# A fourth place for attention probabilities, a seventh addend for GpSimd in six narrow steps, and later projections in an eight-sample U-net block

## What is computed

```
block 0:  x  = x + proj(attention(group_norm(x)))            8 heads of 32 channels
block 1:  a  = group_norm(x) + pos;  gate = sigmoid(conv(silu(conv3x3(silu(conv(a))))))
          sh = group_norm(a);  enh = a * gate
          std = attention(sh, sh, sh)                          8 heads of 32
          mul = [attention(enh, sh, sh)] * 2                   2 heads of 128
          x   = x + group_norm(ff(silu(ff1([std, mul]))))
block 2:  xn = group_norm(x);  x = xn + proj(attention(xn))    8 heads of 32
block 3:  x  = x + proj(attention(group_norm(x)))            1 head of 256
attention: softmax(q k / sqrt(d)) v   over 1024 x 1024 scores a head
```

## Time and profile before

| | us |
|---|---|
| median of 3 runs | 5251.7 (5237.88 to 5256.1) |
| the profiled execution: its time, its span | 5264.05, 5262.3 |
| PE busy | 4914.8 (93%) |
| POOL, DVE, ACT busy | 2868.2 (55%), 3047.0 (58%), 2418.6 (46%) |
| mean granted clock of PE | 0.948 of full |

### The profile page before, as it was taken

One profiled execution on the slowest core, in us unless ns is written; L12 is line 12 of the kernel. 1 busy time (PEld: TensorE's weight loads), 2 busy tenths in 40 slices (PEclk: granted clock), 3 DMA queues, 4 the chain that ended last, 5 costly groups with the idle time before them and its releaser, 6 DMA issues. The chain is left out here.

```text
span 5262.3 us, 62946 instructions
## 1 busy us (share of the span) xinstructions
PE 4914.8 (93%) x22016; PEld 2254.5 (43%) x22016; DVE 3047.0 (58%) x5432; ACT 2418.6 (46%) x4321; POOL 2868.2 (55%) x1649
## 2 busy tenths in 40 slices
PE   7789999999999999999999999999999999999888
PEld 3325334553335533354334633346333463345424
DVE  6455666366773666636665467555666456763462
ACT  3352555435553455524555245552555425553251
POOL 3472567436664466634667357563666535764362
PEclk8899989999999998999999999899989999999988
DMA  3111212021210211102210112201122012110110
GB/s 88 27 35 46 55 37 55 16 60 45 51 37 21 75 42 40 37 26 64 55 43 20 41 49 57 49 13 47 49 51 55 7 53 57 46 46 11 30 36 12
DMA packets 103606, 221.18 MB, mean 42 GB/s; under 512 B 31104, under 2 KB 33408, under 8 KB 103168
## 3 DMA queue, kind: packets, MB, share of 16 engines
q1 hardware_dynamic: 103296, 217.16, 16.0%
HBM read 56.47 MB, written 8.39 MB: 12 GB/s over the span
## 5 line engine op out<-in xcount | busy, mean ns | idle before, releaser
L855 ACT ACTIVATE probs<-bank 128x512 f32<-128x512 f32 x3456 | 1934.5, 599 | 2401.5 <-PE bank L517 2279.4
L958 DVE TENSOR_REDUCE max_cols<-bank 128x1 f32<-128x512 f32 x3456 | 2191.5, 681 | 1367.4 <-PE bank L517 1360.0
L1200 POOL TENSOR_TENSOR probs_added<-probs_added,probs 128x1024 f32<-128x1024 f32 x768 | 1796.8, 2373 | 83.5 <-ACT probs L855 83.4
L517 PE MATMUL bank<-q_stack,k_stack 97*128 97x512 f32 (+1 forms) x3584 | 1674.2, 523 | 63.8 <-DVE max_cols L958 32.1
L517 PE MATMUL bank<-probs,v_tokens 128*32 128x512 f32 (+1 forms) x7168 | 1373.7, 639 | 31.5 <-ACT probs L855 29.9
L1200 POOL TENSOR_TENSOR probs_added<-probs 128x1024 f32<-128x1024 f32 x192 | 454.0, 2370 | 1042.0 <-ACT probs L855 1040.3
L517 PEld LDWEIGHTS bank<-q_stack,k_stack 97*128 97x128 f32 (+1 forms) x3584 | 665.2, 195 | 799.7 <-issue 442.6
L517 PE MATMUL bank<-act,weight_stream 128*128 128x512 f32 x1792 | 937.1, 625 | 38.6 <-ACT act L865 27.4
L1187 POOL TENSOR_TENSOR probs_added<-probs_added,probs 128x512 f32<-128x512 f32 x288 | 368.4, 1279 | 623.5 <-ACT probs L855 622.2
L517 PE MATMUL bank<-high_parts 32*128 32x512 f32 x3072 | 403.7, 513 | 120.1 <-DVE max_cols L958 82.0
L517 PEld LDWEIGHTS bank<-probs,v_tokens 128*32 128x32 f32 (+1 forms) x7168 | 317.0, 122 | 444.4 <-issue 306.2
(11 more groups left out here) (84 smaller groups left out, 2929.9 us busy)
## 6 DMA issues: line engine op xcount, KB each, us to landing
k_stack<-high_parts SPq DMA_DIRECT2D x384, 128.0 KB, 2.4
q_stack<-high_parts SPq DMA_DIRECT2D x768, 64.0 KB, 2.0
weight_stream<-stream_dram SPq DMA_DIRECT2D x32, 768.0 KB, 4.3
k_stack<-low_parts SPq DMA_DIRECT2D x192, 128.0 KB, 2.4
q_stack<-low_parts SPq DMA_DIRECT2D x384, 64.0 KB, 2.0
act<-x_dram SPq DMA_DIRECT2D x8, 1024.0 KB, 6.5
act<-pos_dram SPq DMA_DIRECT2D x8, 1024.0 KB, 5.8
weight_stream<-stream_dram SPq DMA_DIRECT2D x16, 512.0 KB, 3.9
```

What stands on the lines that cost most here:

```text
L517: return nc.tensor.matmul(dst, lhsT, rhs, start=start, stop=stop, **kw)
L855: act.activation(PR[:, m % P_RING, j, :], bank[:, :], ACT.Exp, scale=att.scale).then_inc(reading(key), 1)
L958: dve.tensor_reduce(cols[:, kh, j, qt:qt + 1], bank[:, :], AX.X, ALU.max).then_inc(reading(key), 1)
L1200: pool.tensor_tensor(ADD[:, js, :], one, two, ALU.add).then_inc(p_added, 1)
```

## The change

Three things are changed. P_RING is 4. A table (`places_of_probs`) gives each item the place that was used longest ago, of four places in a narrow attention and of three in a wide one. The fourth place lies where the tile `wide_low` lies, which "m" alone uses, and DVE gets one wait ahead of its first write to it. Then, in all four steps of 0/2 and in steps 1 and 2 of 2/1, POOL adds items 0 to 6 and PE's `sums_narrow` takes item 7 and `probs_added`. That holds where there is work beside, so in turns 1 to 7: 42 steps of the 96 narrow ones. Last, the table of stages is shifted: beside "2", the second norm of block 1 comes three units later, the gate's first convolution between half a unit earlier and one later, the other two 1.5 to 3 units later, and the projections of group 0 three; beside "0" the projections of group 0 come 1.8 units later, and the stacks and values behind them are packed closer.

```diff
-P_RING = 3
+P_RING = 4
-ADDED = 6
+ADDED, ADDED_BESIDE = 6, 7
+        self.added = [ADDED] * self.steps
+    def beside(self, between):
+        for s in {"0": range(4), "2": (1, 2)}.get(self.kind, ()) if between is not None else ():
+            self.added[s] = ADDED_BESIDE
...
-            each("stats", [("a",) + q for q in QUARTERS], 42, 1) + unit("sa1", 0, 2, 44) + unit("sa1", 1, 2, 46.5) + \
-            norm("norm", 47.2, 2.5, "a", "o") + unit("sa2", 0, 3, 54.5) + unit("sa2", 1, 3, 57.5) + \
+            each("stats", [("a",) + q for q in QUARTERS], 41.5, 1.5) + unit("sa1", 0, 2, 43.5) + unit("sa1", 1, 2, 47.5) + \
+            norm("norm", 50.2, 2.5, "a", "o") + unit("sa2", 0, 3, 56) + unit("sa2", 1, 3, 59.5) + \
...
-        out += projections(group(0), 71.1, 1) + stacks(80, 2.3) + values(82.1, 2) + projections(group(1), 109.1, 1.7) + \
+        out += projections(group(0), 74.1, 1) + stacks(82.5, 2.1) + values(84.1, 2) + projections(group(1), 109.1, 1.7) + \
...
-            projections(group(0), 76.8, 1) + stacks(85.5, 2) + values(87, 2) + projections(group(1), 110.1, 1.6) + \
-            narrow_start(88, 121.5, 118, 4)
+            projections(group(0), 78.6, 1) + stacks(87, 1.8) + values(88.6, 1.9) + projections(group(1), 110.1, 1.6) + \
+            narrow_start(87, 121.5, 118, 4)
...
+def places_of_probs():
+    place, prior, last = [], [], [None] * P_RING
+    for m, (att, _) in enumerate(ITEMS):
+        p = min(range(P_RING - att.wide), key=lambda p: -1 if last[p] is None else last[p])
+        place.append(p)
+        prior.append(last[p])
+        last[p] = m
+    return place, prior
...
-        WLO = sb("wide_low", [P, CT, T], F32R)
+        WLO = sb("wide_low", [P, CT, T], F32R, at=pr_at + (P_RING - 1) * 4 * HALF * 4)
...
-                if part < 2:
+                if part < 8 - att.added[s]:
...
-                    for part in range(3):
+                    for part in range(9 - att.added[s]):
...
-                if j == 0 and m >= P_RING:
-                    act.wait_ge(p_used, m - P_RING + 1)
-                    added = added_before(*ITEMS[m - P_RING])
+                if j == 0 and PRIOR[m] is not None:
+                    act.wait_ge(p_used, PRIOR[m] + 1)
+                    added = added_before(*ITEMS[PRIOR[m]])
...
-                    if not 1 <= i < ADDED or j % 2 == 0:
+                    if not 1 <= i < att.added[s] or j % 2 == 0:
```

More of the change, by code:

```diff
@@ L70, in __init__ @@
         self.units = self.steps * self.per
-        self.adds = 7 if self.wide else 2 * (ADDED - 1)
+        self.added = [ADDED] * self.steps
         self.maxima = QT * NH * (1 if self.wide else GROUP)
@@ L80, in head, with adds @@
         return 0 if self.kind == "3" else s // NH
+    def beside(self, between):
+        for s in {"0": range(4), "2": (1, 2)}.get(self.kind, ()) if between is not None else ():
+            self.added[s] = ADDED_BESIDE
+    def adds(self, s):
+        return self.adds0 + (7 * s if self.wide else sum(2 * (n - 1) for n in self.added[:s]))
     def buf(self, s):
@@ L177, in stages @@
         out = proj("1") + norm("pre", 21, 2.5, "e", "a") + each("pos", QUARTERS, 34.8, 1) + [(39, "border", 0)] + \
-            each("stats", [("a",) + q for q in QUARTERS], 42, 1) + unit("sa1", 0, 2, 44) + unit("sa1", 1, 2, 46.5) + \
-            norm("norm", 47.2, 2.5, "a", "o") + unit("sa2", 0, 3, 54.5) + unit("sa2", 1, 3, 57.5) + \
-            tile("sa3", 0, 1, 63.6) + tile("sa3", 1, 1, 66.1) + [(65.9, "sa3 one", 0), (68.4, "sa3 one", 1)] + \
-            each("spatial", QUARTERS, 68.8, 1)
-        out = [(at + (4.8 if name == "apply" and i[0] == "norm" else 0), name, i) for at, name, i in out]
-        out += projections(group(0), 71.1, 1) + stacks(80, 2.3) + values(82.1, 2) + projections(group(1), 109.1, 1.7) + \
+            each("stats", [("a",) + q for q in QUARTERS], 41.5, 1.5) + unit("sa1", 0, 2, 43.5) + unit("sa1", 1, 2, 47.5) + \
+            norm("norm", 50.2, 2.5, "a", "o") + unit("sa2", 0, 3, 56) + unit("sa2", 1, 3, 59.5) + \
+            tile("sa3", 0, 1, 65.6) + tile("sa3", 1, 1, 69.1) + [(67.9, "sa3 one", 0), (71.4, "sa3 one", 1)] + \
+            each("spatial", QUARTERS, 71.8, 1)
+        out = [(at + (3.2 if name == "apply" and i[0] == "norm" else 0), name, i) for at, name, i in out]
+        out += projections(group(0), 74.1, 1) + stacks(82.5, 2.1) + values(84.1, 2) + projections(group(1), 109.1, 1.7) + \
             narrow_start(87, 120.5, 118, 4)
@@ L224, in turns @@
             slots.append((att, Between(g, n, who) if there else None))
+            if att is not None:
+                att.beside(slots[-1][1])
     items = steps = narrow_steps = adds = narrow = restored = 0
@@ L234, in turns @@
         steps += att.steps
-        adds += att.adds * att.steps
+        adds = att.adds(att.steps)
         if not att.wide:
@@ L354, in added_before @@
     if att.wide:
-        return att.adds0 + 7 * (item // 2) + (3, 7)[item % 2]
+        return att.adds(item // 2) + (3, 7)[item % 2]
     s, i = divmod(item, 8)
-    return att.adds0 + att.adds * s + 2 * max(1, i) if i < ADDED else 0
+    return att.adds(s) + 2 * max(1, i) if i < att.added[s] else 0
 NAMES = "eaxomf"
@@ L588, in values_narrow @@
                              i == 0, i == 7, tile_position=(0, D * j))
-                if i < ADDED:
+                if i < att.added[s]:
                     ins.then_inc(p_used, 1)
@@ L595, in sums_narrow @@
                 key = ("sums", att.index, s)
-                if part < 2:
+                if part < 8 - att.added[s]:
                     if part == 0:
                         take(key, True)
-                    sums(PS[tiles[key][0]], narrow_probs(att, s, ADDED + part), part == 0, False).then_inc(p_used, 1)
+                    sums(PS[tiles[key][0]], narrow_probs(att, s, att.added[s] + part), part == 0, False).then_inc(p_used, 1)
                 else:
-                    pe.wait_ge(p_added, att.adds0 + att.adds * (s + 1))
+                    pe.wait_ge(p_added, att.adds(s + 1))
                     sums(PS[tiles[key][0]], ADD, False, True).then_inc(filling(key), 1)
@@ L1095, in _ @@
                     dve.wait_ge(hi_done, count["high"])
+                    if att.kind == "m" and name == "k" and i == (0, 0):
+                        m = max(m for m in range(att.item0) if PLACE[m] == P_RING - 1)
+                        dve.wait_ge(p_used, m + 1)
+                        dve.wait_ge(p_added, added_before(*ITEMS[m]))
                     key = (name, att.index, i)
@@ L1180, in score @@
                     until_read(pool, key)
-                    one, two = (PR[:, (att.item0 + v // 4) % P_RING, v % 4, :] for v in (u - 1, u))
+                    one, two = (PR[:, PLACE[att.item0 + v // 4], v % 4, :] for v in (u - 1, u))
                     if r == 1:
@@ L1193, in score @@
                     m, js = att.item0 + u // 4, slice(j - 1, j + 1)
-                    one, two = PR[:, (m - 1) % P_RING, js, :], PR[:, m % P_RING, js, :]
+                    one, two = PR[:, PLACE[m - 1], js, :], PR[:, PLACE[m], js, :]
                     if i == 1 and j == 1:
```

9 lines of the change are left out of this document (5 added, 4 removed).

## The result

| | before | changed |
|---|---|---|
| median, us (range, runs) | 5244.8 (5232.8 to 5256.1, 4) | 5174.1 (5166.3 to 5180.5, 4) |
| profiled execution: its time, its span | 5264.05, 5262.3 | 5180.53, 5178.8 |

The ratio is 0.9856, with a 95% interval of 0.9832 to 0.9881: 1.4% faster, 71 us between the medians. The forecast was 5169 us, 83 us less than the 5251.7 known then; a fourth time of the kernel before has since moved its median to 5244.8. The two profiled executions differ by 83.5 us, the sum that was forecast, but the experiments show that a part of this is chance.

The account below looks back on a forecast made before the run. PE bound the kernel, by its own instructions and by short waits that pull its clock down. 36 - 15 + 15 + 17 + 30 = 83 us off the 5251.7 median gave 5169, range 5095 to 5238.

Parts of the forecast that it names:

- the exchange of waits in turn 8: Attention 2, turn 8: ACT's waits for POOL go to near 0, and PE waits for `probs_added` in their place.
- A: In 42 steps PE makes one direct sum fewer, 0.855 us each: 36 us gained.
- C: Step 1 of 0/2, unit 66: PE newly waits for POOL's additions, 1.0 to 4.0 us a turn, 15 us lost.
- B: Beside "0": the later projection of "k" fills 2.1 of PE's 3.0 us wait for the norm, 15 us gained.
- D: Step 1 of 2/1: shifted norm and gate give 7 us from shorter waits and 10 from a better clock, 17 in all.
- E: Three narrow attentions without work beside them: the fourth place ends ACT's waits for POOL, 10 us each, 30 in all.
- most is given back at unit 66: Rival, chance 0.13: the wait in 0/2 adds a half-clock stretch, lone attentions gain 5 us each; 33 us gained, 5219.
- the 43 to 55 forecast: Sign in the changed kernel's page: steps 1 of 2/1 should lie between 43 and 55 us.
- as in turn 2: Upper bound for step 1 of 2/1: 48 us gained if the clock behaved in all turns as there, 44.3 us each.
- as in turn 6: Lower bound for step 1 of 2/1: 36 us lost if the clock behaved in all turns as there, 56.2 us each.
- the lower bound of 7: Least gain in us forecast for each lone attention from the fourth place: half of PE's waits.
- The check on DVE: POOL's added work should not slow DVE's maxima, 627 to 695 ns; the rival that VectorE slows down had chance 0.02.

Follow-up runs that it names:

- the two kernels whose sums are shown above: The changed kernel with the stages beside "2" as before, 5158.7 us, ratio 0.9845 to the kernel before; and the changed kernel itself, 5174.1 us.
- The run with five items: Changed kernel with six items on POOL in step 1 of 0/2 and five in attentions with no work beside them: 5127.5 us, 0.9771 to the kernel before.

## Why the prediction was right

The forecast of 5169 us is within 5 us of the median. The gain was forecast at 83 us and measured at 71; the two times lie closer than that because the median of before came out 7 us lower. The mechanisms were found in their places: 336 records fewer, POOL 193 us busier (198 forecast), a wait for POOL at unit 66 of 0/2 in all seven turns (1.0 to 2.4 us), 0.57 us ahead of "k" (with 3.0 before), and the exchange of waits in turn 8. But most terms were off in size, and their errors cancel: that the total came so close is in part luck.

| term | forecast | what the runs show |
|---|---|---|
| A, 42 sums | +36 | +36, if all are worth what seven in step 3 of 0/2 are (6.1 us) |
| C, the wait at unit 66 | -15 | -17 to -20 |
| B, the wait ahead of "k" | +15 | about +20 in the traces, 8 ± 17 in time |
| (not foreseen) closer packing, step 3 of 0/2 | 0 | +8.7 in the traces, more in time, not explained |
| D, shifts beside "2" | +17 | nothing in time, some 10 in the traces |
| E, the fourth place | +30 | +14 in the trace with the rest of the change (16 ± 18 in time), 0 alone in time |

The likely sums, 36 - 19 + 20 + 9 + 5 + 14 = 65, stand against 71 measured. They are read from single traces for the most part. By time alone three things are clear: the seventh item with the place is worth some 33 us, the table of stages 38, and of the table nearly all is the part beside "0", "k" and packing together.

*C and B* come from the length of step 2 of 0/2 over seven turns, from the sums of its windows in fourteen traces:

| | "k" at 76.8 | "k" at 78.6 |
|---|---|---|
| six items at unit 66 | 306.3, 302.1, 311.5, 308.0 | 287.9, 280.3, 286.3, 285.7 |
| seven items | 314.9, 319.5, 319.8 | 301.8, 300.9, 292.9 |

The rows' means are 307.0, 285.1, 318.1 and 298.5. The later "k" gives 22 us with six items and 20 with seven. The seventh item costs 11 and 13 here, although it saves seven sums, 6 us, so C is 17 to 20. PE's waits for POOL themselves were only 10.8 us of it. The prediction had put the clock's part of B and C against each other at nothing. The table shows that each had one of its own. The wait ahead of "k" fell by 3.00 - 0.57 = 2.4 us, 17 in seven turns, so 3 to 5 of its 20 to 22 are the clock's. At unit 66 it is 6 to 9 us, where the half level of turn 2 held 21 us with the wait and 6 without. The length of the wait doesn't order it: in the changed kernel the clock of step 2 was 0.84 with a wait of 2.41 us (turn 1) and 0.77 with 1.61 (turn 2), where it had fallen ahead of the wait. So the rival "most is given back at unit 66" had a right mechanism and too large a price.

*D* failed as the prediction put it: "I take it to shrink by 1 us" and "10 from a somewhat better clock". PE's waits in step 1 of 2/1 did shrink, from 5.1 to 3.1 us in turn 2: the gate's 1.7 are gone and 1.1 of those for the probabilities, and 0.5 for the variance and 0.3 more for the maxima came. Step 1 of 2/1 is indeed 27 us shorter (355.1 in the mean of six traces, 328.4 in eight), and in the changed kernel each turn lay between 45 and 51 us, inside the 43 to 55 forecast. But the prediction read that step alone. Of the 27 us, some 16 are taken back in steps 2 and 3 (10.3 and 7.1 in the two kernels whose sums are shown above), and the length of step 1 varies by 20 us between two executions of one kernel. That the clock varies on its own shows in turns 2 and 6 of the earlier trace rows: PE waits 5.1 and 4.4 us in them, and the turn with fewer waits has the clock of 0.72. That also makes the bounds of this term, "as in turn 2" and "as in turn 6", results of chance and not of the code. The 10 us left are a hint at most: the two traces that have seven items and the old stages in 2/1 read 1109 and 1125 us for the whole of it.

*E* failed in "PE waits for `probs_added` in its place. The last sum moves from 5141.79 to about 5131": the waits moved as said, but I took most of POOL's idle time ahead of the steps for time that can be had. POOL idled 5.80, 5.85 and 3.33 us, and idles 3.67, 3.67 and 3.24 ahead of the same steps now:

```profile
4976.86 2.35 POOL L1231 TENSOR_TENSOR probs_added<-probs 128x1024 f32<-128x1024 f32 x1 [3.67 <-ACT probs L881]
...
5004.74 2.36 POOL L1231 TENSOR_TENSOR probs_added<-probs 128x1024 f32<-128x1024 f32 x1 [3.67 <-ACT probs L881]
...
5032.17 2.36 POOL L1231 TENSOR_TENSOR probs_added<-probs 128x1024 f32<-128x1024 f32 x1 [3.24 <-ACT probs L881]
```

The two hold each other: PE waits for POOL's last addition, the scores behind that wait come late, and POOL then waits for ACT's next item. So 4.4 of 15 us were to be had, and an attention gave 2 to 7 us, most of them less than the lower bound of 7. The run with five items shows that the 30 us were there, for who takes work off POOL in these attentions.

The check on DVE held. The common maximum takes 627, 681 and 694 ns (least, median, most) under 193 us more of POOL's work, as in the earlier trace rows. The Trainium skill, GPSIMD Engine Reference, section 8 (Key points), names contention of GpSimd with VectorE instructions that have two inputs in SBUF. The change can't show more of that rule than before, since these instructions take 752, 796 and 1676 ns, unchanged, and stand where nothing more is added. But POOL does add in wide attentions too, and there the trace agrees, in both kernels: of the 32, the 14 that took 1.50 to 1.68 us all ran beside a POOL addition, and of the 17 that took 0.75 to 0.80 us all but one ran beside none.

## What to carry to other kernels

Work moved from the busiest engine to an idle one is worth its time on the first one (here 0.86 us a sum) only where the second ends before it is waited for; look for the steps where it also has other work, and leave these out. Where the helper is idle for a part of the time but its chain of additions is what ends a stage, give it less and not more: taking one item off POOL in three lone attentions gave 31 us, nearly as much as all 42 sums. Trace the same kernel twice before you explain a difference: two executions of it differed by 20 us in one kind of step, and an edit's effect must be summed over the steps behind it as well, since a later place moves work across the border.

## What had not been expected of the hardware

- PE's clock falls after short waits, and can stay down while PE is nearly always busy. In the changed kernel, turn 2, it was at half at 1208.26, after waits of 1.45, 0.45 and 0.43 us, at full at 1216.51, and at half again behind the wait of 2.61. It then stayed at half for 21 us of step 2, in which PE waited 1.61 and 0.57 us and little else. The Trainium skill, TensorE: Matmul & The Clock Gate, section "A second HAM failure mode: psum-queue depth-cycling", tells of a clock that oscillates when PE idles briefly between groups of matmuls; the trace agrees that the clock goes up and down within a step, here in float32 and with waits for other engines.
- The same program, with the same work on the other engines, spans 5215.1 us at a mean clock of 0.957 and 5262.3 at 0.948. Where the half level starts in 2/1 is not the same from run to run; in 0/2 and the lone attentions it nearly is.
- A wait of 0.54 us twice in a step is enough to matter: with both gone, step 3 of 0/2 is 1.2 us shorter in each turn, at a clock of 1.00 in both.
